# A gated graph network: layer 1 multiplies x itself, W1 goes into the gate weights, and twelve pairs of the adjacency stay on chip for a second product

## The reference, cut to what matters

```python
def ggc(x, adj, W, wih, whh, bih, bhh):
    m = adj @ (x @ W)
    gi, gh = m @ wih.T + bih, x @ whh.T + bhh
    i_r, i_z, i_n = split(gi, 3); h_r, h_z, h_n = split(gh, 3)
    r, z = sigmoid(i_r + h_r), sigmoid(i_z + h_z)
    n = tanh(i_n + r * h_n)
    return (1 - z) * n + z * x

h  = relu(ggc(x, adj, W1, ...))          # layer 1
h2 = relu(ggc(h, adj, W2, ...))          # layer 2
x  = layernorm(x + h2)
# second network: weights that halve with the rank of a neighbour, at most 100 of them
mask = (adj != 0); rank = cumsum(mask, axis=1); deg = rank[:, -1:]
k = minimum(deg, 100); pos = rank - (deg - k)
w = mask * where(pos > 0, 0.5 ** (k - pos), 0)
out = layernorm(x + w @ (x @ weight) + bias)
```

## Time and profile before

| | |
|---|---|
| median of 3 runs | 357.27 us (357.25 to 358.22) |
| the profiled execution: its span | 356.2 us |
| PE busy | 336.1 us, 94% |
| DVE busy | 302.3 us, 85% |
| ACT busy | 180.3 us, 51% |
| bytes moved | 111.10 MB, mean 312 GB/s |
| TensorE clock granted | 1.00 of full speed in nearly every stretch |

### The profile page before, as it was taken

The page is one execution under the profiler, slowest core; times in us unless marked ns, Lnnn a source line. Parts: engine busy times, 40 slices in busy tenths (PEclk is TensorE's granted clock), DMA queues, the critical chain, the costliest instruction groups (busy, mean ns, idle before and its releaser), DMA issues.

```text
span 356.2 us, 6673 instructions
## 1 busy us (share of the span) xinstructions
PE 336.1 (94%) x2488; PEld 154.6 (43%) x2488; DVE 302.3 (85%) x510; ACT 180.3 (51%) x235; POOL 24.8 (7%) x32
## 2 busy tenths in 40 slices
PE   1999999999999999999999989999999999989992
PEld 1333233333333333333333324544444445879992
DVE  0589989898999999878985666899898999888996
ACT  0202404132041230367466447877895969676993
POOL 2000000000000000000000001202020202022044
PEclk9999999999999999999999999999999999999999
DMA  7999999999998999999998999999999996000012
GB/s 249 413 409 409 409 410 406 410 408 397 407 343 302 411 403 345 310 337 332 309 324 294 379 391 410 344 326 346 341 369 349 395 399 242 17 3 2 2 33 89
DMA packets 32720, 111.10 MB, mean 312 GB/s; under 512 B 3632, under 2 KB 6192, under 8 KB 32688
## 3 DMA queue, kind: packets, MB, share of 16 engines
q1 hardware_dynamic: 31824, 109.20, 81.1%
q10 hardware_dynamic: 864, 1.48, 1.2%
HBM read 109.62 MB, written 1.05 MB: 311 GB/s over the span
## 4 chain that ended last, share of the span: by engine, by line
PE 80%; DMA 11%; DVE 4%; issue 2%; ACT 1%; POOL 1%; POOLq 0%; ACTq 0%; DVEq 0%
PE m_acc L446 42%; PE out L446 15%; DMA stream<-in_adj_t 10%; PE out L555 7%; PE gate_ps L503 4%; PE gate_ps L510 3%; PE gate_ps L555 3%; PE gate_ps L526 2%; PE m_acc L555 2%; DMA w<-in_w 2%; PE gate_ps L438 1%; PE m_acc L478 1%; POOL rstd L843 1%; PE out L488 1%; DVE stream L1155 0%
## 5 line engine op out<-in xcount | busy, mean ns | idle before, releaser
L446 PE MATMUL m_acc<-stream,s_in 128*64 128x512 f32 x512 | 126.0, 607 | 1.6 <-DMA stream<-in_adj_t 1.0
L903 DVE TENSOR_SCALAR codes<-stream 128x1024 uint8<-128x1024 f32 x117 | 76.4, 685 | 3.6 <-DMA stream<-in_adj_t 3.5
L446 PE MATMUL out<-stream,s_mid 128*64 128x512 f32 x272 | 69.3, 595 | 1.5 <-DMA stream<-in_adj_t 1.5
L446 PEld LDWEIGHTS m_acc<-stream,s_in 128*64 128x64 f32 x512 | 33.8, 137 | 65.7 <-issue 52.5
L446 PE MATMUL m_acc<-stream,s_mid 128*64 128x512 f32 x240 | 54.2, 597 | 0.3 <-DMA stream<-in_adj_t 0.3
L843 POOL TENSOR_TENSOR rstd<-var,mhalf 128x4 f32<-128x4 f32 x16 | 23.0, 1436 | 327.7 <-DVE var L1058 327.7
L952 DVE SCALAR_TENSOR_TENSOR codes<-codes,run 128x384 uint32<-128x384 uint32 (+2 forms) x56 | 43.0, 768 | 1.9
L947 DVE TENSOR_TENSOR run<-run,codes 128x768 uint16<-128x768 uint16 (+2 forms) x55 | 41.5, 754 | 1.8
L638 ACT ACTIVATE m_high<-m_acc 64x512 f32<-64x512 f32 x13 | 7.7, 593 | 59.2 <-PE m_acc L446 45.8
L446 PEld LDWEIGHTS out<-stream,s_mid 128*64 128x64 f32 x272 | 19.1, 137 | 40.3 <-issue 39.9
L670 ACT ACTIVATE rz<-gate_ps,b_rz 128x256 f32<-128x256 f32 x32 | 13.4, 469 | 42.8 <-PE gate_ps L510 42.8
(11 more groups left out here) (139 smaller groups left out, 378.6 us busy)
## 6 DMA issues: line engine op xcount, KB each, us to landing
stream<-in_adj_t SPq DMA_DIRECT2D x204, 512.0 KB, 6.1
x_res<-in_x_pairs SPq DMA_DIRECT2D x8, 128.0 KB, 7.2
out_nodes<-stream SPq DMA_DIRECT2D x8, 128.0 KB, 2.0
hx<-in_x_pairs ACTq DMA_DIRECT2D x1, 512.0 KB, 7.2
const<-in_consts ACTq DMA_DIRECT2D x1, 358.0 KB, 6.6
hx<-in_x_pairs ACTq DMA_DIRECT2D x2, 128.0 KB, 6.1
hx<-in_x_pairs ACTq DMA_DIRECT2D x1, 256.0 KB, 8.8
bias_b<-in_bias SPq DMA_DIRECT2D x1, 128.0 KB, 5.4
```

The source lines that it names most:

```text
L446: last = nc.tensor.matmul(to[D * u:D * (u + 1), :], state[:, t * D:(t + 1) * D], stream[:, n % SLOTS, u * CW:(u + 1) * CW], start=start[u] ...
L903: nc.vector.tensor_scalar(edges(p // 2, b, 2 * (p % 2), 2), stream[:, n % SLOTS, :], 0.0, None, ALU.not_equal).then_inc(mask_made, 1)
```

## The change

Nine things change together.

1. Layer 1 multiplies `adj` by x itself: `s_in` is loaded from a second copy of x in node order (`x_nodes`, 1 MB, four transfers on ACT's queue). `x_w1` and `xw_copy` go away. W1 is multiplied into the gate weights of layer 1 once (`fold` on PE, `copy_folded` on DVE, in chunk 0).
2. `hx` (1 MB) is now loaded on SP's queue, among the pairs: 128 KB after (0, 9), 128 KB after (0, 14), 256 KB after (1, 6), 512 KB after (3, 2). The constants shrink from 358 KB to 262 KB, W1 from 64 KB to 16 KB.
3. Twelve pairs of pass 1 (`HELD`: four of chunk 0, two each of chunks 1 to 4) do not land in a slot but in a part of `codes` that is not written yet (8 places), and stay there until a second product with `s_mid` (`product_held`). These run after the ordinary product at the places of `HELD_AT`: two in chunk 1, four in chunk 2, two each in chunks 3, 4 and 5. The twelve reloads of pass 2 go away: 192 transfers of pairs in place of 204.
4. `KEPT` takes in chunk 0 (a fifth copy and add in pass 1, a fifth identity product in pass 2), with other banks and other places for the copies (`KEEP_AT`).
5. `ALONG_PAIRS`, the pairs beside each chunk of layer 2, is 7, 8, 9, 9, 9, 10 (was 8, 10, 12, 12, 11, 11).
6. Chain tiles: 15 tiles early in place of 12, with the three added ones of the first part in chunk 6 and of the second part at the end of chunk 7. The late tiles are `CHAIN` = 7, 7, 4, 3, 3, 3, 4, 1 (was 5, 5, 5, 4, 4, 4, 4, 1). The limit after tile (3, 0) moves from t = 3 to t = 2.
7. Four masks of chunks 4 and 5 go from DVE to ACT.
8. `to_x1s` and some constants are half as wide.
9. The order of the pairs in chunk 3 is another.

```diff
-KEPT = range(1, 5)
+KEPT = range(5)
+HELD = [(0, 0), (0, 1), (0, 2), (0, 3), (1, 2), (1, 3), (2, 4), (2, 5), (3, 6), (3, 7), (4, 8), (4, 9)]
+HELD_AT = {(1, 13): (0, 0), (1, 15): (0, 1), (2, 10): (0, 2), (2, 11): (0, 3), (2, 13): (1, 2),
+           (2, 15): (1, 3), (3, 13): (2, 4), (3, 15): (2, 5), (4, 13): (3, 6), (4, 15): (3, 7),
+           (5, 13): (4, 8), (5, 15): (4, 9)}
+X_AT = ((0, 9), (0, 14), (1, 6), (3, 2))
-CHAIN_EARLY = ({3: (11, 13, 15), 4: (4, 7, 10, 13), 5: (4, 7, 10, 14), 6: (4,)},
-               {6: (10, 11, 12, 13, 14, 14), 7: (2, 4, 6, 8, 10, 12)})
+CHAIN_EARLY = ({3: (11, 13, 15), 4: (4, 7, 10, 13), 5: (4, 7, 10, 14), 6: (2, 4, 6, 8)},
+               {6: (10, 11, 12, 13, 14, 14), 7: (2, 4, 6, 8, 10, 12, 13, 14, 15)})
-ALONG_PAIRS = {1: 8, 2: 10, 3: 12, 4: 12, 5: 11, 6: 11}
+ALONG_PAIRS = {1: 7, 2: 8, 3: 9, 4: 9, 5: 9, 6: 10}
-CHAIN = [chain_tiles(*x) for x in ((0, 5), (5, 10), (10, 15), (15, 19), (19, 23), (23, 27), (27, 31),
+CHAIN = [chain_tiles(*x) for x in ((0, 7), (7, 14), (14, 18), (18, 21), (21, 24), (24, 27), (27, 31),
...
+        def pair_at(n):
+            if n in SLOT:
+                return stream[:, SLOT[n], :]
+            at = (HELD.index(LOADS[n]) % HOLDS * NCH + NCH - 2) * BLK
+            return codes[:, at:at + 2 * BLK].bitcast(F32)
...
-            def x_w1(c):
-                ...
+            def fold():
+                pe.wait_ge(consts_loaded, 16)
+                pe.wait_ge(w1_in, 16)
+                for at, w in ((slice(0, P), w_rz_m), (slice(P, P + D), w_n_m)):
+                    last = nc.tensor.matmul(rz_ps[0:D, at], w_1t, w, start=True, stop=True)
+                last.then_inc(fold_done, 1)
...
+            def product_held(b, q):
+                i = HELD.index((b, q))
+                pe.wait_ge(s_mid_made, q // 2 + 1)
+                pair(LOAD_AT[b, q], q, s_mid, m2_bank(b), [i == 0] * 2, i + 1 == HELD_END[b])\
+                    .then_inc(held_used, 1)
...
-                        if 0 < q < NP - 2:
-                            x_w1(q // 2 + 1)
-                        pe.wait_ge(xw_copied, q // 2 + 1)
+                        pe.wait_ge(nodes_in[X_PART[q // 2]], 16)
                     product1(b, PAIRS[b][q])
+                    if (b, q) in HELD_AT:
+                        product_held(*HELD_AT[b, q])
```

More of the change, by code:

```diff
@@ L40 @@
 ROOT = 0.125
-SET_POOL = 14
+SET_POOL = 13
 HW = CW // 2
@@ L255, in build @@
         w_max = sb("w_max", [P, 4], F32)
-        unscale = sb("unscale", [P, 1], F32)
+        scalars = sb("scalars", [P, 3], F32)
+        unscale, code_bias, start_bias = [scalars[:, i:i + 1] for i in range(3)]
         w_s, centre_s = kept[0:D, 1, 0:D], kept[:, 1, D:2 * D]
@@ L459, in product1 @@
                     if first:
-                        if b == 5:
-                            pe.wait_ge(to_sup_made, 4)
+                        if b == 2:
+                            pe.wait_ge(to_sup_made, 2)
                         if b in M2_AFTER:
                             pe.wait_ge(m2_kept, KEPT.index(M2_AFTER[b]) + 1)
-                    last = pair(n, q, s_mid, m2_bank(b), [first] * 2, q == twice[-1] and b in KEPT)
+                    last = pair(n, q, s_mid, m2_bank(b), [first] * 2, False)
                 last.then_inc(pair_used, 1)
+            def product_held(b, q):
[3 more added lines that the diff above has]
+                    .then_inc(held_used, 1)
             def product2(s, q):
@@ L469, in product2 @@
                 n = LOAD_AT[g, q]
-                first = s >= 3 and q == 2 * TRI[ch]
+                first = s >= 3 and q == PASS2[ch]
                 pe.wait_ge(s_mid_made, q // 2 + 1)
@@ L510, in gates @@
                         last = nc.tensor.matmul(to[e * D:(e + 1) * D, HW:CW],
-                                                w_n[layer][rows, part * D:(part + 1) * D],
+                                                w_n[layer][rows, :],
                                                 mx[rows, e * HW:(e + 1) * HW],
@@ L1018, in _ @@
                         weight_max()
+                    if b == 0 and q == 11:
+                        copy_folded()
                     if b == 0 and q == 13:
```

204 lines of the change are left out of this document (108 added, 96 removed).

## The result

The changed kernel takes 367.9 us (median of four runs, 367.39 to 370.16) where the kernel before takes 357.75 beside it: a ratio of 1.031, with an interval from 1.0281 to 1.0338. It is 10.2 us slower. 364.6 was forecast, with 361.5 to 367.5 around it: the time lies 0.4 us above that, inside the wider range up to 368.5. Of the two profiled executions, 367.40 and 357.27 us, the spans are 365.4 and 356.2: 9.2 us are inside the span and 0.9 outside. Run again later on one chip, with 4 runs of after and 13 of before, the ratio is 1.0305 [1.0262 to 1.0349].

A forecast was written before the change was run, and what follows sets the result against it. Transfers bound early pass 1, then PE up to the turn; in pass 2 each chunk loops through PE, DVE and ACT. Terms sum to +7.3 us: span 356.2 to 363.5, time 364.6, forecast range 361.5 to 367.5 (52%).

The forecast's parts named there:

- t = 3: Step of layer 2 in pass 2: 15.9 us where it was 18.06, so -2.2.
- x times W1: Pass 1 before pair (1, 0): removing 6.3 us of PE matmuls gains nothing, because PE waits for pairs there.
- x loads: Before pair (1, 0): 0.37 MB more to load, +1.5 us, within 0.9 to 4.0.
- Twelve products in pass 1: Products moved from pass 2: 10.3 us on PE with 0.6 to spare, so pass 1 gets 9.7 us longer.
- DVE in chunk 7: Chunks 6 and 7: six more early tiles and one kept add on DVE, partly hidden, +0.5 us (0 to 3).
- The turn: Between the passes: two more short tiles before layer 2's first combine; the following gates at 220.6 for 220.26, +0.3 us.
- t = 2: Step of layer 2 in pass 2: 16.35 us for 15.79, +0.6, with PE waiting 2.3 us.
- t = 4, 5, 6: Later steps of pass 2: 15.9, 14.9 and 14.8 us, so -1.6, -0.7 and -0.8.
- From span to time: Outside the profiled span: the median of the runs lies 1.07 us above it, so span 363.5 gives 364.6.
- the loops of pass 2 cost nothing: Rival on pass 2: DVE and ACT keep up with shorter steps; +1.9 us, 359.2, chance 20%.
- the faster one: Rival at the turn: PE's 2.1 us of waits for pairs go as well; -1.3 us, 356.0, chance 12%.
- DVE falls behind in chunks 6 and 7: Slower rival: late codes and slots there, and a longer wait at the turn; +3 more, 367.6 us, chance 11%.

The follow-up runs named there:

- sems: The kernel before with 13 more semaphores that nothing uses; 356.87 us against 356.89, ratio 0.9998.
- again: The changed kernel run once more, unedited, beside the kernel before on one chip; 368.2 us against 357.16.
- x_alone: The kernel before with only the part of the change on x and W1, including hx on SP's queue; 358.76 us, ratio 1.0052.
- expand_late: The kernel before with one DVE expansion moved from the end of t = 6 to behind the combine in t = 7; 356.16 us, ratio 0.9977.
- early: The changed kernel with the last early tiles of chunk 7 placed sooner; 366.57 us, ratio 1.0265.
- half2: The changed kernel with only the six held pairs of chunks 2 to 4, pairs per step dealt 7, 8, 10, 11, 12, 10; 368.35 us, ratio 1.0331.
- node3: The changed kernel with node behind three pairs in place of four at t = 2 and 3; 366.58 us, ratio 1.0262.
- chainb: The changed kernel with pass 2's tiles dealt to the steps as before the change; 367.21 us, ratio 1.0297.

## Why the prediction was wrong, and what in it was right

The direction was right, and pass 1 came out within 0.6 us (10.75 for 10.2). What failed is how much of it pass 2 gives back, and the step of the sum in which it failed is t = 3. The change takes twelve products out of pass 2 and puts in one identity product, 9.3 us of PE. From the gates of chunk 7 to the end the forecast gave back 4.4 of them (0.3 + 0.6 - 2.2 - 1.6 - 0.7 - 0.8); the two profiled executions have 2.8 (157.6 for 160.4 us), the two typical ones, sems and again, only 0.7 (158.3 for 159.0). By the prediction's own steps:

- **x times W1**, nothing: right (x_alone).
- **x loads**, +1.5: 1.24 at pair (1, 0). That pair starts at 46.2 to 46.6 in before, sems and expand_late, and at 47.3 to 47.8 in the changed kernel and its variants, so the term is known to some 0.4. The text put it between the bytes, 0.9, and 4.0. The Trainium skill (DMA: Bandwidth & Descriptors, Issuing engines are not separate DMA queues) says that transfers of different engines run on the same 16 DMA engines and interleave, by which the queue makes no difference. x_alone has 1.3 there and 1.9 over the whole kernel, because the 512 KB behind (3, 2) also delay pairs that are only just in time. In the whole change the held products fill that wait: PE is busy for 29.88 of 30.00 us from 46 us on, and for all of the 124 us behind. Nothing here separates the queue from the place in it: no run had the pieces at these places on ACT's queue.
- **Twelve products in pass 1**, +9.7, and **DVE in chunk 7**, +0.5: 10.75 together, and the second term is the one mis-sized: 0.95 by the run early, so 9.8 for the products. The six products of chunks 0 and 1 cost 3.8 beyond the other six (half2), since they fill waits for pairs, with hx now among the pairs.
- **The turn**, +0.3 over gates and t = 1 together: +0.38 in the profiled pair, but +1.2 in sems and again (24.64 for 23.45). The wait of t = 2's gates for make_x1s, foreseen as 1.4, is 1.23. The text's own terms give 220.3, not 220.6, and those of t = 2 add up to 16.15, not 16.35; the rest is some 0.2 us that it doesn't name.
- **t = 2**, 16.35 with a wait of 2.3 for make_x1s: 16.51 with 2.08.
- **t = 3**, 15.9, so -2.2: this is the step that failed inside the span. It took 16.89, and 18.44 in again; against a typical 17.49 of before that is -0.6 to +0.95. The prediction let PE go to node as soon as the new state was ready, 7.3 after gates, and the state was ready then (7.4 in node3). It did not see that with three pairs of the old sum ahead, the fourth pair in front of node belongs to the next sum, whose identity product needs the bank that combine frees; before the change it stood behind node. Node came 10.0 after the gates. node3 puts node first and gives 0.6 of it back against the profiled execution, 2.15 against again. The rest is the baseline of 18.06: sems and x_alone have 17.49, with nothing changed in this step. The prediction also had no term for the clock, which in again made this step 1.5 us longer.
- **t = 4, 5, 6**, 15.9, 14.9, 14.8: 15.91, 15.06, 14.78. The sigmoids 3 to 4 us behind the gates are there, 3.99 at t = 3 and 3.95 at t = 4.
- **Tail**, 0: +0.3.
- **From span to time**, 1.07: 2.0 for after at the place of the first comparison, 1.8 for both kernels in the later ones. This 0.9 is not the change, and with it the forecast of 363.5 for the span becomes 365.5. The sum was also made against an execution of before with a span of 356.2, where the medians of later runs are 355.0 to 355.6. Two of its terms, the turn and t = 3, took waits for single pairs as things that the change could win, and a typical run has fewer of them.

The time is 3.3 us above the 364.6: 1.1 by t = 3, 0.8 by the other steps (0.5 of it DVE in chunk 7), 0.8 by the time outside the span, and 0.6 because the median of the four runs is longer than the profiled one. That it is no more is luck, since the sum started from a long execution of before: from 355.4, the 7.3 us give a span of 362.7, where again has 366.35.

Of the rivals, "the loops of pass 2 cost nothing" is refuted by the steps t = 2 and 3 and by chainb, the faster one by the waits at the turn, which turned from waits for pairs into waits for combine. "DVE falls behind in chunks 6 and 7" gave the nearest number, 367.6, but by luck: of its reasons only the late combine of chunk 7 is seen, with 1 us of its 3; no wait for a slot came with it (PE waits 0.39 us for a pair at the turn, before 0.89 and more).

Not tested alone are the four masks that went to ACT, the fifth kept sum and the other order of the pairs in chunk 3.

## What to carry to other kernels

Before you move work between two passes, ask of each pass which engine ends it: the pass that gets the work pays in full if that engine is its bound (here less where it filled waits: 3.8 for 5.2 us), and the one that loses it gives back only what the other engines' loops allow. When a table deals accumulations to steps, look at which product is the first of a new sum and what it waits for; the order of that product against the loop's own matmul decides whether the wait is free. And take the baseline of a sum from several executions, since one may hold waits that the next has not.
